# Sixteen weight chunks moved into attention 1, none left in a block loop, GpSimd's order in the shared stage

## The reference

```python
# attention 0: kv = ctx @ W_k.T + b; out = xn @ kv; sim = out @ kv.T * scale
#              sim = layernorm over the last axis * gamma + beta; softmax(sim)
# FFN 0: 8 experts of 192, 2 for each token, and a shared expert of 1024
# attention 1: 16 heads of 32 in 4 groups that share keys and values from ctx;
#              softmax(q k' * scale) v, then @ Wc.T + bc
# FFN 1: 16 experts of 352 with biases, 6 for each token, and a shared expert of 704
# an expert: (silu(x @ w1.T + b1) * (x @ w3.T + b3)) @ w2.T + b2, weighted per token
```

## Time and profile before

| | us |
|---|---|
| median of 3 runs | 2461.47 (2459.92 to 2462.63) |
| the profiled execution | 2456.83 |
| its span | 2454.9 |
| TensorE busy | 1958.3 (80%) |
| VectorE busy | 1235.9 (50%) |
| GpSimd busy | 1025.3 (42%) |
| ScalarE busy | 798.7 (33%) |
| mean granted TensorE clock | 0.898 of full speed |

### The profile page before, as it was taken

The page is one execution under the profiler, slowest core; times in us unless marked ns, Lnnn a source line. Parts: engine busy times, 40 slices in busy tenths (PEclk is TensorE's granted clock), DMA queues, the critical chain, the costliest instruction groups (busy, mean ns, idle before and its releaser), DMA issues. The chain is left out here.

```text
span 2454.9 us, 36235 instructions
## 1 busy us (share of the span) xinstructions
PE 1958.3 (80%) x10825; PEld 1590.0 (65%) x10825; DVE 1235.9 (50%) x2637; ACT 798.7 (33%) x1279; POOL 1025.3 (42%) x819
## 2 busy tenths in 40 slices
PE   5426888786777547878887887899999879999995
PEld 2215676665555425555554676779998778989995
DVE  7943545232222169988886656544443323434442
ACT  4423111112323226756765311113332222323331
POOL 4755555462333347766652110014342333434331
PEclk9658899898898759989998999999999989999998
DMA  8886865789777452222212000084648787574444
GB/s 278 271 269 211 274 206 171 253 252 331 188 227 180 93 145 42 48 34 37 44 20 69 35 28 26 1 343 85 158 80 288 235 270 247 91 225 84 79 81 107
DMA packets 129377, 374.69 MB, mean 153 GB/s; under 512 B 20440, under 2 KB 24408, under 8 KB 124024
## 3 DMA queue, kind: packets, MB, share of 16 engines
q1 hardware_dynamic: 78808, 259.02, 32.6%
q0 software_dynamic: 33600, 79.73, 17.5%
q10 hardware_dynamic: 16800, 33.76, 3.8%
HBM read 211.96 MB, written 151.84 MB: 148 GB/s over the span
## 5 line engine op out<-in xcount | busy, mean ns | idle before, releaser
L1535 PE MATMUL ps<-f_wb,f_xThi 128*128 x2088 | 545.0, 343 | 43.0 <-issue 33.6
L1639 POOL DMA_INDIRECT y_scratch<-f_yo,f_rows x150 | 238.5, 1590 | 525.7 <-ACT f_yo L1379 325.2
L1535 PEld LDWEIGHTS ps<-f_wb,f_xThi 128*128 128x128 f32 x2088 | 377.6, 195 | 71.9 <-issue 63.7
L1535 PE MATMUL ps<-f_wb,f_xTlo 128*128 x1044 | 350.7, 336 | 0.0
L1554 PE MATMUL ps<-f_wb,f_hThi 128*128 (+1 forms) x822 | 281.7, 424 | 19.4 <-DVE f_hTlo L1850 19.4
L684 POOL TENSOR_TENSOR a_elo<-a_e,a_ehi 128x768 f16<-128x768 f32 x128 | 217.4, 1707 | 141.8 <-ACT a_ehi L740 139.7
L1618 POOL DMA_INDIRECT f_xg<-xn_scratch,f_rows x150 | 159.8, 1065 | 197.8 <-PE ps L1519 145.2
L1868 DVE TENSOR_TENSOR f_g<-ps,f_bb 128x352 f32<-128x352 f32 x111 | 58.3, 525 | 343.8 <-PE ps L1535 343.8
L1379 ACT ACTIVATE f_yo<-ps,f_share 128x512 f32<-128x512 f32 x150 | 103.1, 688 | 310.3 <-PE ps L1554 169.8
L1535 PEld LDWEIGHTS ps<-f_wb,f_xTlo 128*128 128x128 f32 x1044 | 203.9, 195 | 0.0
L1462 PE MATMUL ps<-f_xhi,f_w13hi 128*128 128x512 f32 x448 | 177.3, 396 | 27.0 <-POOL f_w13lo L1588 27.0
(11 more groups left out here) (237 smaller groups left out, 3872.8 us busy)
## 6 DMA issues: line engine op xcount, KB each, us to landing
f_wb<-w_scratch SPq DMA_DIRECT2D x16, 2816.0 KB, 12.2
f_wb<-w_scratch SPq DMA_DIRECT2D x24, 1536.0 KB, 15.0
w_scratch<-f_stage_up SPq DMA_DIRECT2D x34, 1024.0 KB, 5.3
f_stage_raw<-in_f_w_dram SPq DMA_DIRECT2D x36, 768.0 KB, 7.2
w_scratch<-f_stage_down SPq DMA_DIRECT2D x136, 128.0 KB, 2.3
w_scratch<-a_stage_up SPq DMA_DIRECT2D x14, 1024.0 KB, 5.3
a_stage_raw<-in_f_w_dram SPq DMA_DIRECT2D x14, 768.0 KB, 7.1
xn_scratch<-f_xn ACTq DMA_DIRECT2D x32, 256.0 KB, 3.4
```

Source lines behind the costliest of these rows:

```text
L1535: mm = pe.matmul(out, xt[:, b % 2, k, :], weights(at, w, k, low), start=(m == 0), stop=(m == 3 * KD - 1))
L1639: pool.indirect_dma_start(y_d, bass.IndirectOffsetOnAxis(ap=rows_of[:, b:b + 1], axis=0), yo[:, b % 3, :], None, bounds_check=ROWS + P - 1 ...
```

## The change

- The constants: 9 chunks in attention 0, 3 early and 28 in FFN 0's shared stage, none in its block loop, and the last 16 (`LATER`) in attention 1.
- `high` and `low` can do single pieces, with a count on each high piece; the number of up buffers of a `Stage` is a parameter (`ups`).
- In attention 1 a `Stage` with one up buffer. Two chunks per unit in units 0 to 3 and 12 to 15: in steps 0, 1, 2 and 4, 5, 6 ScalarE makes a high piece after the exponentials; one step later GpSimd makes the low piece after its residue. SyncE stores the first chunk after the query strips and the second after the maxima, and loads the next but one.
- In FFN 0's shared stage GpSimd makes the next pair's w13lo before the chunks of the last two steps of a pair, and w2lo after the chunks of the first two.
- The zero rows are not written. FFN 1 loads two whole down tiles, 96 rows and the bias row as separate transfers (5 for 3), and the last product contracts over 97 rows. The four padding blocks are waited for at the end of attention 0.

```diff
-AT_ONCE = 14
-EARLY = 5
-SHARED = 29
-EVERY = 4
+AT_ONCE = 9
+EARLY = 3
+SHARED = 28
+LATER = 16
...
+            def high(self, eng, copy, i, pieces=range(3)):
+
+                for w in pieces:
+                    if w == 0:
+                        eng.wait_ge(self.raw_in[i % 2], 16 * (i // 2 + 1))
+                        if i >= self.ups:
+                            eng.wait_ge(self.up_out[i % self.ups], 16 * (i // self.ups))
+                    if w < 2:
+                        copy(self.part(i, w, 0), self.source(i, w)).then_inc(self.hi_done, 1)
+                    else:
+                        if i >= 1:
+                            eng.wait_ge(self.down_out, 16 * STRIPS * i)
+                        copy(self.down[:, 0, :], self.raw[:, i % 2, 1024:1536]).then_inc(self.hi_done, 1)
+
+            def low(self, eng, i, pieces=range(3)):
+
+                for w in pieces:
+                    eng.wait_ge(self.hi_done, 3 * i + w + 1)
...
-                for e in range(E1):
-                    sp.dma_start(g["w2_d"][1][e, rest:P, HC1 - 1, :], zero[rest:P, :]).then_inc(zero_out, 16)
...
-                sp.wait_ge(zero_out, 16 * (4 + E1))
...
+        stage = g["Stage"](ctx, "a1_stage_", ups=1)
...
+        SLOTS = [(u, n) for u in (*range(GROUPS), *range(UNITS - GROUPS, UNITS)) for n in range(2)][:LATER]
...
+        def split_step(u, j, lag):
+
+            n, w = divmod(j - lag, 4)
+            i = chunk_of(u, n) if w < 3 else None
+            return (i, (w,)) if i is not None else (0, ())
...
+                def keep(u, n):
+                    i = chunk_of(u, n)
+                    if i is not None:
+                        stage.store(sp, i, *later(i))
+                        if i + 2 < LATER:
+                            stage.load(sp, i + 2, *later(i + 2))
...
                         load(u + 2, (grp + 2) % GROUPS)
                         strips(u + 2, (grp + 2) % GROUPS)
+                    keep(u, 0)
                     if has_maxima:
                         maxima(u + 1, (grp + 1) % GROUPS)
+                    keep(u, 1)
...
+                        stage.low(pool, *split_step(u, j, 1))
...
                         act.activation(ehi[:, j % 4, :, :], ps[:, 2 * (j % 2):2 * (j % 2) + 2, :],
                                        ACT.Exp).then_inc(exp_done, 1)
+                        stage.high(act, act.copy, *split_step(u, j, 0))
...
-    LOADS = 3
-    LAST_K = P if BIASED else REST
+    LOADS = 5 if BIASED else 3
+    LAST_K = REST + 1 if BIASED else REST
...
-                    for i in last_pieces(b, 0):
-                        stage.high(act, act.copy, i)
-                    for i in last_pieces(b, 2):
-                        stage.store(act, i, *piece(i))
-                        if AT_ONCE + i + 2 < len(g["PREPARED"]):
-                            stage.load(act, i + 2, *piece(i + 2))
...
+                pair_lo(0)
+                for p in range(PAIRS):
+                    for s in range(8 * p, 8 * p + 2):
+                        both(s)
                     for h in range(2):
                         pool.wait_ge(w2hi_ready, 2 * p + h + 1)
...
+                    for s in range(8 * p + 2, 8 * p + 6):
+                        both(s)
+                    if p + 1 < PAIRS:
+                        pair_lo(p + 1)
+                    for s in range(8 * p + 6, 8 * p + 8):
+                        both(s)
```

More of the change, by code:

```diff
@@ L155, in load @@
                 sp.dma_start(self.raw[:, i % 2, :], a[f"f{layer}_w"][chunk, :, :]).then_inc(self.raw_in[i % 2], 16)
[L157 to L174, removed]
+            def high(self, eng, copy, i, pieces=range(3)):
[13 more added lines that the diff above has]
+                    eng.wait_ge(self.hi_done, 3 * i + w + 1)
+                    if w < 2:
+                        eng.tensor_tensor(self.part(i, w, 1), self.source(i, w), flt(self.part(i, w, 0)),
+                                          ALU.subtract)
+                    else:
+                        eng.tensor_tensor(self.down[:, 1, :], self.raw[:, i % 2, 1024:1536],
+                                          flt(self.down[:, 0, :]), ALU.subtract).then_inc(self.lo_done, 1)
             def store(self, sp, i, layer, chunk):
@@ L209, in cross_attention_0 @@
         count = sb(ctx, "a0_count", [P, P + 1 + NT], I32)
[L210 removed]
+        zero = sb(ctx, "a0_zero", [P, D + MOE[1]["E"]])
         stage = g["Stage"](ctx, "a0_stage_")
@@ L291, in _ @@
                 sp.wait_ge(b2_out, 16)
-                for i in range(2):
-                    sp.wait_ge(stage.up_out[i], 8 * AT_ONCE)
-                sp.wait_ge(stage.down_out, 16 * STRIPS * AT_ONCE)
+                sp.wait_ge(zero_out, 16 * 4)
+                stage.stored(sp, AT_ONCE)
             PARAMS, SCALES = 16 * 4, 16 * 4
@@ L573, in batches, with chunk_of, later @@
                 unit(u, grp, u + 2 < UNITS, u + 1 < UNITS, B - 2)
+        SLOTS = [(u, n) for u in (*range(GROUPS), *range(UNITS - GROUPS, UNITS)) for n in range(2)][:LATER]
+        def chunk_of(u, n):
+            return SLOTS.index((u, n)) if isinstance(u, int) and (u, n) in SLOTS else None
+        def later(i):
+            return g["PREPARED"][g["LAST"] + i]
+        def split_step(u, j, lag):
+            n, w = divmod(j - lag, 4)
+            i = chunk_of(u, n) if w < 3 else None
+            return (i, (w,)) if i is not None else (0, ())
         with nc.Block() as block:
@@ L614, in _ @@
                 strips(1, 1)
+                for i in range(2):
+                    stage.load(sp, i, *later(i))
                 maxima(0, 0)
+                def keep(u, n):
[4 more added lines that the diff above has]
+                            stage.load(sp, i + 2, *later(i + 2))
                 def unit(u, grp, has_prepare, has_maxima, wc_batch):
@@ L1254, in _ @@
                 if layer == 0:
-                    for i in range(2):
-                        sp.wait_ge(stage.up_out[i], 8 * (len(g["PREPARED"]) - AT_ONCE))
-                    sp.wait_ge(stage.down_out, 16 * STRIPS * (len(g["PREPARED"]) - AT_ONCE))
+                    stage.stored(sp, g["LAST"] - AT_ONCE)
                 added(sp, BLOCKS)
@@ L1597, in _, with pair_lo @@
                         stage.low(pool, i)
-                for p in range(PAIRS):
+                def pair_lo(p):
                     if BIASED and p == PAIRS - 1:
@@ L1605, in _, with both @@
                         split_lo(h)
+                def both(s):
+                    for i in prepared(s):
+                        stage.high(pool, pool.tensor_copy, i)
+                        stage.low(pool, i)
+                pair_lo(0)
+                for p in range(PAIRS):
+                    for s in range(8 * p, 8 * p + 2):
+                        both(s)
                     for h in range(2):
@@ L1611, in _ @@
                         pool.sem_inc(raw_free[h], 1)
-                    for s in range(8 * p, 8 * p + 8):
-                        for i in prepared(s):
-                            stage.high(pool, pool.tensor_copy, i)
-                            stage.low(pool, i)
+                    for s in range(8 * p + 2, 8 * p + 6):
[4 more added lines that the diff above has]
+                        both(s)
                 def gather(b):
@@ L1891, in _ @@
                         turned_rows(b + 1)
-                    for i in last_pieces(b, 1):
-                        stage.low(dve, i)
                 turned(BLOCKS - 1)
```

38 lines of the change are left out of this document (22 added, 16 removed).

## The result

The changed kernel takes 2528.7 us (median of 4, 2518.7 to 2536.8) where the kernel before takes 2462.1 beside it: a ratio of 1.0267, 95% interval 1.0228 to 1.0306. It is slower, as forecast, but by 66.7 us and not by 32.5. The time lies just inside the range (2460 to 2530); the loss is twice the forecast one.

A forecast was written before the change was run, and what follows sets the result against it. Each stage has its own limit, and the chunk work touches four of them. Terms: attention 0 -30, FFN 0 -29 and -22, attention 1 +114, FFN 1 0; sum +33, so 2489.8 us profiled, 2494 median, range 2460 to 2530.

The forecast's parts named there:

- The loop through the up buffer: Attention 1: each chunk's first high piece waits for the previous up store to land; intervals 146.2 and 136.8, term +114.
- The signs: Attention 1: ScalarE idle 6 to 10 us before 15 chunks' first casts, units 0-3 and 12-14 of 37 to 42 us.
- SyncE's queue in attention 1: Attention 1: the key cast was counted as 0.6 us of ScalarE work in the loop, with no wait for its load.
- I take off 7: Attention 1: 7 us off the 120.8 difference, since VectorE, some 4 us behind at each end, catches up in the stalls.
- Attention 0: Nine chunks for 14 and no zero rows remove VectorE's 25.4 us gap before FFN 0: term -30, bounds -25 and -35.
- the 5 net that I took: Attention 0: VectorE gains 7 us late, where GpSimd is quiet, against 2 lost early, where GpSimd starts sooner.
- FFN 0: Fewer early chunks and reordered low halves give -29 up to the block loop; no chunks in that loop give -22.
- Start: FFN 0's shared stage: TensorE can start at 204.6 instead of 215.5 with three early chunks on GpSimd, -10.9.
- The 3.3 for pair 3's low down-weights: FFN 0's shared stage: three chunks ahead of pair 3's low down-weights make TensorE wait for them, +3.3 us.
- the landing does not bind: Rival, attention 1: ScalarE's wait for the up store is covered, only GpSimd's share costs, 28; time 2408; chance 0.08.
- GpSimd limits FFN 0: Rival: reordered chunks delay low down-weights and the gather stays late; FFN 0 gives 15 instead of 51, 2530; chance 0.13.
- half the loss is caught up: Rival, attention 1: 14 intervals at 18 us, so no change, 2463; chance 0.07.

The follow-up runs named there:

- e2: The changed kernel with a second up buffer in attention 1, SyncE's order kept: 2456.3 us, ratio 0.9984 to the kernel before.
- e4: The changed kernel with the up buffer's store issued before the four down strips in attention 1: 2504.7 us, ratio 1.0176 to the kernel before.
- e1: The changed kernel with the next unit's keys loaded before the second chunk's store and raw load on SyncE in attention 1: 2511.6 us, ratio 1.0204.
- e9: e8 with twelve chunks in attention 0 for nine and thirteen in attention 1 for sixteen: 2404.8 us, ratio 0.9789 to the kernel before.
- e6: e3 with GpSimd's order in FFN 0's shared stage as it was before the change: 2424.8 us, ratio 0.9866 to the kernel before.
- e3: The changed kernel with both a second up buffer and the keys' load first in attention 1: 2417.5 us, ratio 0.9827 to the kernel before.
- e8: e3 with a third raw buffer in attention 1, raw loads issued after the query rows or the maxima: 2406.4 us, ratio 0.9793.
- e5: The changed kernel without high and low pieces in attention 1, all transfers kept in the same order: 2404.9 us, ratio 0.9772 to the kernel before.
- e7: e3 with the 16 blocks of zero rows again written and waited for in attention 0: 2418.4 us, ratio 0.9826 to the kernel before.
- e10: e8 unchanged, timed once more: 2402.7 us, ratio 0.9785 to the kernel before.

## Why the prediction was right in sign and wrong in size

**The loop through the up buffer: right.** e2 takes it away and 72 us go, e4 shortens it and the time follows. With the keys out of the way (e1) the intervals sum to 151.2 and 138.2, where the prediction had 146.2 and 136.8: its terms, each from a row, were 6 short over 14 intervals. The up store landed in 5.3 at the median, as in attention 0. The 5.3 holds the 0.8 that the raw load behind the store costs: the prediction had this load only in its upper bound, although its row already included it.

For a transfer issued by GpSimd the Trainium skill, DMA: Bandwidth & Descriptors, "Anatomy of one DMA", gives 2.0 us plus the bytes over 436 GB/s, an estimate of 4.4 us for this megabyte. The traces agree for a store from SyncE with no raw load behind it (4.5); with one, the 5.3 of the rows is right. The signs came nearly as forecast: 14 waits (the prediction said 15) of 6.9 to 11.7 us (it said 6 to 10); the units take 33 to 47 us where it gave 37 to 42.

**The failed step: SyncE's queue in attention 1.** The prediction followed the store on SyncE into the loop and never asked what stands behind it. It counted the key cast at 0.6 us of work and put the wait before it at nothing, without a reason. But the keys' load of the next unit now sits behind `keep(u, 1)`: behind a store that waits for GpSimd's last low piece, and behind 2.25 MB of traffic. Against e1, the profiled execution has the first seven intervals longer by 7.6 (158.9 for 151.2) and the other seven by 3.7, and 5.4 more between the last first piece of unit 3 and unit 5, 17 in all; by the medians of the runs it is also 17.

**The second failed step: "I take off 7".** VectorE was to catch up in the stalls, so that the ends of the stretches would be shorter. They are longer even with the keys first: from the last first piece of unit 3 to unit 5's first exponential 41.9 us for 35.9, and 33.8 for 30.1 from unit 15's to FFN 1. Instead of 7 less they cost 9.7 more, an error of 16.7. In e1 the account closes: 114 + 6.4 + 16.7 = 137.1, measured 136.7. For the changed kernel it is 114 + 6.4 + 16.7 + 17 + 6 (unit 8) = 160, measured 159.7. The query rows behind the second chunk's transfers explain at least part of the longer end: TensorE waits 6.6 for them in unit 4 of e1, and 2.7 at most in any of units 0 to 4 before. What the lower granted clock of the stage adds there (0.80 for 0.85 in unit 4 of e1) was not separated.

**Why 80 in the traces and 67 by the medians.** The profiled execution of the changed kernel was its slowest of four, 8 above the median, and that of the kernel before was 5 below its own. Against the forecast of +33 the traced difference is what the steps must explain.

**Attention 0: right, -27.5 for -30.** VectorE's multiply by gamma is at 682 ns at the median where it was 1091 (by line, min/median/max ns):

```profile
L457 DVE TENSOR_TENSOR a_y<-a_y,a_gamma x16: 680/682/1751, 46.4 to 122.6; 128x512 f32<-128x512 f32 x16
```

Yet VectorE ends at 128.8 where it ended at 131.4, a gain of 2.6 and not the 5 net that I took. The late gain was larger than forecast, 9.4 for 7: the last two of the four batches take 39.0 us for 48.4. The early loss was larger still, 6.8 for 2. Most of it is one instruction over 4 columns, beside GpSimd's first chunk; in the kernel before, and in the changed one:

```profile
21.92 2.45 DVE L115 TENSOR_SCALAR rstd<-inv 128x4 f32<-128x4 f32 x1
```

```profile
21.27 7.56 DVE L110 SCALAR_TENSOR_TENSOR vraw<-mdif,vraw 128x4 f32<-128x4 f32 x1
```

In the batches before, either takes 0.17 at most. GpSimd works without a break from 21.10 to 28.80, and this instruction ends at 28.83; in the kernel before, GpSimd paused for 0.09 us at 24.34, and VectorE's ended at 24.37. The changed kernel and nine of the ten made from it have one such instruction of 7.0 to 7.6 us in their profiles. That of e2 has none, and there attention 0 takes 122.1, against 129.2 to 131.6 in the others with nine chunks.

By the Trainium skill, SBUF — State Buffer, "Who interferes with whom", a VectorE instruction with two SBUF inputs and a GpSimd one that reads SBUF wait for each other. The traces agree: the multiply by gamma, with both inputs in SBUF, takes 678 to 1751 ns in the kernel before, and the scaling ahead of it (L442), whose data input is PSUM, 801 to 811. The price is e9's: 5.8 us for three chunks more.

**FFN 0: right.** Start -11.2 for -10.9, and e6 shows the order's share, 10.2 of wait before pair 3. The 3.3 for pair 3's low down-weights did not come: TensorE has no wait for GpSimd over 2 us in this stage. The first gather is issued 367 us into the stage, 369 foreseen. In the block loop six of 38 intervals now exceed 6.2 us, one for each load that falls among them; what the intervals above 5.7 have in excess of it falls from 47.7 to 28.9.

**The rivals.** That the landing does not bind is refuted by the 14 waits for it. That GpSimd limits FFN 0 is refuted by the 53.5 us that its two parts gained. That half the loss is caught up needed intervals of 18 us; they are 18.1 to 24.7, 21.5 in the mean.

## What to carry to other kernels

When work is inserted on a transfer queue, list what the queue issues next and who waits for that, before pricing the inserted work: an in-order queue that waits for a slow engine hands this wait on to transfers that had nothing to do with it. A buffer whose loop (compute, issue, land) is 20 us long needs two copies if it is asked for every 12; space for the second was found in a tile dead by then, and with the queue order it turned 67 us lost into 41 gained (e3), and into 53 with the third raw buffer (e8). A wait taken away behind a longer one pays little until the longer is gone too: 17 and 39 us for the same edit. A large load issued right behind a store delays the store's landing, here by 0.8 us: where the landing is waited for, issue something else first.

## What the runs showed that I had not expected

Transfers alone cost 36 us in the profile (e5, without unit 8's 6) and less at the medians, in a stage whose DMA engines are busy 38% of the time in the changed kernel. Nearly all of it falls in the five units in which the keys' cast waits. Three chunks on GpSimd, wholly inside VectorE's time and ahead of its end, cost 5.8 us of it, 1.9 each.

Unit 8, which has no chunk, takes 23.8 or 29.4 us in profiles of otherwise alike kernels (29.4 in the changed kernel, e2, e5 and e7; 25.2 in e9 and e10). Two stretches of the changed kernel's, and the first of them in e1, with TensorE's granted clock in the column before the last two:

```profile
1118.37:1139.62 21.25, 14.90 (x133) 10.55 (x132) 16.15 (x29) 17.02 (x20) 15.29 (x10) 0.92 0.30 44
1139.62:1146.45 6.83, 5.80 (x25) 3.22 (x26) 3.19 (x9) 0.00 (x0) 1.93 (x2) 0.51 0.11 31
```

```profile
1106.84:1128.10 21.26, 17.01 (x152) 11.86 (x152) 18.50 (x35) 17.03 (x20) 15.25 (x10) 0.92 0.27 41
```

In the long one TensorE has fallen behind after 21 us, by 19 products, and then the clock drops to its lower level (1.2 GHz) for 6.8 us; in e1 it stays at full speed to the unit's end. What makes TensorE fall behind first is open.
